# One core, cross-attention and a soft mixture of experts: queries as two products (x by Wq, then by turned Wk, two heads side by side) in place of one product with both weights multiplied per head

## What is computed

```
h   = layernorm(x)
q   = h @ Wq;  k = ctx @ Wk;  v = ctx @ Wv          (16 heads of 64)
x   = x + softmax(q k^T / 8) v @ Wo
x   = x + softmoe(layernorm(x))                     (64 experts x 32 slots)
```

## Time and profile before

| | us |
|---|---|
| median of 3 runs (lowest, highest) | 438.74 (438.14, 440.42) |
| the profiled execution, its own time | 439.33 |
| its span in the profile | 437.5 |
| first scores of half 0 / of half 1 / of half 2 start at | 14.92 / 57.40 / 104.41 |

### The profile page before, as it was taken

One profiled execution on the slowest core, in us unless ns is written; L12 is line 12 of the kernel. 1 busy time (PEld: TensorE's weight loads), 2 busy tenths in 40 slices (PEclk: granted clock), 3 DMA queues, 4 the chain that ended last, 5 costly groups with the idle time before them and its releaser, 6 DMA issues.

```text
span 437.5 us, 7430 instructions
## 1 busy us (share of the span) xinstructions
PE 423.5 (97%) x2994; PEld 385.7 (88%) x2994; DVE 331.7 (76%) x608; ACT 245.4 (56%) x413; POOL 160.4 (37%) x89
## 2 busy tenths in 40 slices
PE   6999999999999999999999999999999999899997
PEld 4788899999999999889999998899999888788987
DVE  2777757766786768767898689978988999659870
ACT  2575565675466456645663766456656565534641
POOL 2509900506050305031707053617140342456740
PEclk8999999999999999999999999999999999999999
DMA  8211020114011001210011011001000000196000
GB/s 232 74 51 15 4 82 17 21 63 114 14 23 61 19 13 14 72 18 14 13 72 20 12 14 70 19 12 15 0 20 14 9 4 18 38 254 192 1 1 22
DMA packets 15198, 19.05 MB, mean 44 GB/s; under 512 B 4042, under 2 KB 10970, under 8 KB 15164
## 3 DMA queue, kind: packets, MB, share of 16 engines
q1 hardware_dynamic: 13294, 15.98, 14.4%
q10 hardware_dynamic: 1870, 2.60, 2.1%
HBM read 18.32 MB, written 0.26 MB: 42 GB/s over the span
## 4 chain that ended last, share of the span: by engine, by line
PE 76%; DVE 11%; ACT 5%; issue 2%; POOL 2%; DMA 2%; POOLq 1%; ACTq 0%
PE turned L691 15%; PE scores L675 8%; PE acc L713 8%; PE acc L711 8%; PE acc L712 8%; PE scores L681 8%; PE scores L678 8%; PE misc L728 3%; DVE pT_l L1366 3%; DVE small L1356 3%; PE misc L753 2%; ACT prob L1114 2%; PE misc L595 2%; DMA wk_sb<-in_L_xattn_Wk_dram 2%; ACT pT_h L1107 1%
## 5 line engine op out<-in xcount | busy, mean ns | idle before, releaser
L1107 ACT CAST pT_h<-turned 125x512 fp32r<-125x512 f32 x168 | 95.2, 591 | 122.7 <-PE turned L691 122.0
L1366 DVE TENSOR_TENSOR pT_l<-turned,pT_h 125x512 fp32r<-125x512 f32 x168 | 112.3, 687 | 65.5 <-ACT pT_h L1107 64.6
L1356 DVE TENSOR_REDUCE small<-scores 128x1 f32<-128x500 f32 x168 | 108.4, 674 | 6.4 <-PE scores L681 6.0
L691 PE MATMUL turned<-ident,prob 128*125 128x128 f32 x672 | 94.4, 276 | 3.7 <-DVE pT_l L1366 3.5
L691 PEld LDWEIGHTS turned<-ident,prob 128*125 128x125 f32 x672 | 87.5, 187 | 11.2 <-DVE pT_l L1366 5.5
L711 PE MATMUL acc<-pT_h,ctx_nh 125*128 125x256 f32 (+1 forms) x288 | 94.1, 327 | 0.0
L1114 ACT ACTIVATE prob<-scores,small 128x1500 f32<-128x1500 f32 x56 | 85.0, 1518 | 13.0 <-DVE small L1359 12.6
L713 PE MATMUL acc<-pT_h,ctx_nl 125*128 125x256 f32 (+1 forms) x288 | 86.5, 300 | 0.0
L712 PE MATMUL acc<-pT_l,ctx_nh 125*128 125x256 f32 (+1 forms) x288 | 86.3, 300 | 0.0
L675 PE MATMUL scores<-ctx_th,qk_h 128*128 128x500 f32 x168 | 67.9, 404 | 1.4 <-ACT prob L1114 1.4
L681 PE MATMUL scores<-ctx_th,qk_l 128*128 128x500 f32 x168 | 65.4, 389 | 0.0
(11 more groups left out here) (188 smaller groups left out, 544.0 us busy)
## 6 DMA issues: line engine op xcount, KB each, us to landing
ctx_raw<-in_ctx_dram SPq DMA_DIRECT2D x7, 750.0 KB
rbc<-rden_row SPq DMA_DIRECT2D x15, 128.0 KB, 3.1
rbc<-rden_row SPq DMA_DIRECT2D x8, 192.0 KB, 3.0
eb<-in_L_ffn_expert_b_dram SPq DMA_DIRECT2D x4, 256.0 KB, 5.5
ctx_raw<-in_ctx_dram ACTq DMA_DIRECT2D x3, 224.0 KB
wq_sb<-in_L_xattn_Wq_dram ACTq DMA_DIRECT2D x1, 512.0 KB, 5.0
wv_sb<-in_L_xattn_Wv_dram ACTq DMA_DIRECT2D x1, 512.0 KB, 7.0
wo_sb<-in_L_xattn_Wo_dram ACTq DMA_DIRECT2D x1, 512.0 KB, 8.1
```

Of the source, the lines that this page charges most:

```text
L691: last = tr(turned[0:CK, m, 128 * c:128 * c + 128], prob[u][:, CK * j:CK * j + CK], ident[:, :])
L1107: nc.scalar.copy(pT_h[0:CK, PLACES[g // NT % 2][t], CPB * k:CPB * k + CPB, :], turned[0:CK, (KB * u + k) % 2, :].rearrange("p (c r) -> p c ...
L1356: m = v.tensor_reduce(bankmax[:, u, k:k + 1], scores[:, k, 0:KW], AX.X, ALU.max)
L1366: v.tensor_tensor(pT_l[0:CK, place, dst, :], turned[0:CK, (KB * u + k) % 2, :].rearrange("p (c r) -> p c r", c=CPB), pT_h[0:CK, place, dst ...
```

## The change

Wk is turned (with the scale folded in) and Wq stays as it is. The queries come from two products: `make_qT` makes x by Wq for a pair of heads (128 rows, 112 columns), a copy brings it to SBUF, and `make_qk` multiplies each half of 64 rows by the turned Wk of its head; the two heads of a pair use the upper and the lower half of the array and write to two banks. The rounds are pairs 0-1, 2-3 and 4-7, three in place of four. The queries of the other batches are made in the same two steps: `ahead_queries(j)` (three products), a high and a low part taken by ACT and DVE (`hi_queries`, `lo_queries`), then `ahead_heads(j)` (three pairs of products of 64 rows), and `copy_heads(j)`. They start in step 4 of half 0 and end in step 5 of half 1. Before `ahead_queries(0)`, and before `ahead_heads` in steps 2 to 4 of half 1, TensorE waits for a count of `ctxT_lo`, the semaphore of `lo_ctx`. Wk is loaded first and whole by ACT's queue, Wq in two halves; two filler products (`keep_busy`) stand after the turning of Wk. `turn_weight(wv_sb, 1)` and its copy move from step 1 to step 2. The core of the diff:

```diff
-        wqk, wqk_at = take("wqk", [D, HEADS, D])
+        wq_sb, wqk_at = take("wq_sb", [D, INNER])
+        wkT, _ = take("wkT", [128, HEADS // 2, D])
...
+        QK_PAIRS = ((0, 2), (2, 4), (4, 8))
+
         def rounds_of_qk(t):
 
-            return min(4, -(-(-(-128 * (t + 1) // T)) // 4))
+            heads = -(-128 * (t + 1) // T)
+            return 1 + sum(heads > 2 * j1 for _, j1 in QK_PAIRS[0:-1])
+
+        def qk_banks(r):
+
+            j0, j1 = QK_PAIRS[r]
+            two = turned if r == 0 else misc
+            return two[:, :, 0:PT * (j1 - j0)].rearrange("p m (h b t) -> p b h m t", b=2, t=T)
+
+        def heads_of(ap, r):
+
+            j0, j1 = QK_PAIRS[r]
+            return ap[:, 2 * j0:2 * j1, :].rearrange("p (h m) t -> p h m t", m=2)
...
             sp.dma_start(x_sb[:, :, :], x_v).then_inc(x_in, 16)
-            sp.dma_start(wk_sb[0:DH, :], Wk[0:DH, :]).then_inc(wk_in, 16)
+            sp.dma_start(wq_sb[0:DH, :], Wq[0:DH, :]).then_inc(wq_in, 16)
...
+                    pool.wait_ge(qk_lo, len(QK_PAIRS))
+                    pool.wait_ge(qk_cp, len(QK_PAIRS))
...
-                pool.wait_ge(setup_act, 5)
-                pool.wait_ge(setup_dve, 3)
+                pool.wait_ge(wq_in, 32)
+                pool.wait_ge(setup_act, 1)
+                pool.wait_ge(setup_dve, 1)
                 pool.wait_ge(xnT_dve, 2)
-                gp.tensor_tensor(wqk_h[:, :, :], wqk[:, :, :], zero[:, :].unsqueeze(2).broadcast_to([D, HEADS, D]),
-                                 ALU.add).then_inc(wqk_hi, 1)
+                zeros = zero[:, :].broadcast_to([128, INNER])
+                wkT_cols = [w[:, :, :].rearrange("p j d -> p (j d)") for w in (wkT, wkT_h, wkT_l)]
+                gp.tensor_tensor(wq_h[:, :], wq_sb[:, :], zeros, ALU.add)
+                gp.tensor_tensor(wkT_cols[1], wkT_cols[0], zeros, ALU.add).then_inc(wsplit_hi, 1)
                 gp.tensor_tensor(xa_h[:, 0:PT], xnT[:, 3 * PT:4 * PT], zero[:, :].broadcast_to([D, PT]), ALU.add)
                 gp.tensor_tensor(xa_h[:, PT:NA], xnT[:, PT:3 * PT], zero[:, :].broadcast_to([D, 2 * PT]),
                                  ALU.add).then_inc(xa_hi, 1)
-                pool.wait_ge(wqk_hi, 1)
-                gp.tensor_tensor(wqk_l[:, :, :], wqk[:, :, :], wqk_h[:, :, :].bitcast(F32),
-                                 ALU.subtract).then_inc(wqk_lo, 1)
+                pool.wait_ge(wsplit_hi, 1)
+                gp.tensor_tensor(wq_l[:, :], wq_sb[:, :], wq_h[:, :].bitcast(F32), ALU.subtract)
+                gp.tensor_tensor(wkT_cols[2], wkT_cols[0], wkT_cols[1].bitcast(F32),
+                                 ALU.subtract).then_inc(wsplit_lo, 1)
...
+            def make_qT(j0, j1, k):
+
+                for j in range(j0, j1):
+                    last = mm(bank(k)[:, PT * (j - j0):PT * (j - j0) + PT], wq_sb[:, 128 * j:128 * j + 128],
                               xnT[:, 0:PT], start=True, stop=True)
-                last.then_inc(qk_pe, 1)
-
-
-            def ahead_head(h, m):
-
-                o = misc[:, m, 0:NA]
-                mm(o, wqk_h[:, h, :], xa_h[:, :], start=True, stop=False)
-                mm(o, wqk_h[:, h, :], xa_l[:, :], start=False, stop=False)
-                mm(o, wqk_l[:, h, :], xa_h[:, :], start=False, stop=True).then_inc(ahead_pe, 1)
+                last.then_inc(setup_pe, 1)
+
+            def make_qk(r):
+
+                j0, j1 = QK_PAIRS[r]
+                two = turned if r == 0 else misc
+                for j in range(j0, j1):
+                    for m in range(2):
+                        p = slice(DH * m, DH * m + DH)
+                        last = mm(two[:, m, PT * (j - j0):PT * (j - j0) + PT], wkT[p, j, :], qT[p, j, :],
+                                  start=True, stop=True)
+                        if j == j1 - 1:
+                            last.then_inc(qk_pe, 1)
+
+            def ahead_queries(j):
+
+                o = misc[:, 1, 0:NA]
+                cols = slice(128 * j, 128 * j + 128)
+                mm(o, wq_h[:, cols], xa_h[:, :], start=True, stop=False)
+                mm(o, wq_h[:, cols], xa_l[:, :], start=False, stop=False)
+                mm(o, wq_l[:, cols], xa_h[:, :], start=False, stop=True).then_inc(aq_pe, 1)
+
+            def ahead_heads(j):
+
+                i = j % 2
+                pe.wait_ge(aq_lo, j + 1)
+                for n, (w, q) in enumerate(((wkT_h, qa_h[i]), (wkT_h, qa_l[i]), (wkT_l, qa_h[i]))):
+                    for m in range(2):
+                        p = slice(DH * m, DH * m + DH)
+                        last = mm(misc[:, m, 0:NA], w[p, j, :], q[p, :], start=(n == 0), stop=(n == 2))
+                        if n == 2:
+                            last.then_inc(ahead_pe, 1)
...
             pe.wait_ge(ident_ready, 1)
             keep_busy(2)
-            pe.wait_ge(wq_in, 16)
-            turn_weight(wq_sb, 0, S0)
-            turn_weight(wq_sb, 1, S1)
-            pe.wait_ge(wk_in, 32)
+            pe.wait_ge(wk_in, 16)
             turn_weight(wk_sb, 0, S2)
             turn_weight(wk_sb, 1, T0)
+            keep_busy(2)
             pe.wait_ge(xn_ready, 1)
-            turn_xn(0, 1)
+            turn_xn(0, 1, ACC)
+            pe.wait_ge(wq_in, 32)
+            pe.wait_ge(xnT_dve, 1)
+            make_qT(0, 2, T1)
             turn_ctx(0, 0, 1, first=True)
-            pe.wait_ge(setup_act, 3)
+            pe.wait_ge(setup_act, 2)
             pe.wait_ge(setup_dve, 1)
-            head_pairs(wqT, wkT, 0, T1, S0)
+            make_qk(0)
             turn_ctx(0, 1, 0, first=True)
-            pe.wait_ge(setup_act, 4)
-            pe.wait_ge(setup_dve, 2)
-            pe.wait_ge(xnT_dve, 1)
-            make_qk(0, ACC)
             pe.wait_ge(ctxT_lo, 1)
             turn_ctx(0, 2, 1, first=True)
...
                 q = (b - 4) // 2
-                if b == 1 and t == 0:
-                    pe.wait_ge(wqk_lo, 1)
-                    pe.wait_ge(xa_lo, 1)
-                    ahead_head(0, 0)
-                    ahead_head(1, 1)
-                if b == 1 and 1 <= t <= 5:
-                    pe.wait_ge(ahead_act, 2 * t + 2)
-                    ahead_head(2 * t + 2, 1)
-                if b == 1 and t == 5:
-                    pe.wait_ge(ctxT_lo, KB * (b + 2))
-                    ahead_head(13, 0)
+                if b == 1 and t <= 5:
+                    if 2 <= t <= 4:
+                        pe.wait_ge(ctxT_lo, KB * (b + 1) + t - 1)
+                    ahead_heads(t + 2)
...
+                if b == 1 and t <= 4:
+                    pe.wait_ge(ahead_act, t + 3)
+                    ahead_queries(t + 3)
...
                     if first:
                         if t == 0:
-                            make_qk(1, M0)
-                            head_pairs(wqT, wkT, 2, T0, T1)
+                            make_qT(2, 4, ACC)
                             pe.wait_ge(qk_lo, 1)
                             pe.wait_ge(qk_cp, 1)
+                            make_qT(4, 8, T0)
+                            pe.wait_ge(setup_act, 3)
+                            make_qk(1)
                             pe.wait_ge(xn_ready, 2)
-                            turn_xn(1, NQ)
+                            turn_xn(1, NQ, T1)
                         if t == 1:
-                            pe.wait_ge(xnT_dve, 2)
                             pe.wait_ge(wvo_in, 32)
                             turn_weight(wv_sb, 0, ACC)
                             pe.wait_ge(qk_lo, 2)
                             pe.wait_ge(qk_cp, 2)
-                            turn_weight(wv_sb, 1, M0)
-                            make_qk(2, M1)
+                            make_qk(2)
                         if t == 2:
-                            pe.wait_ge(setup_dve, 4)
-                            make_qk(3, M0)
-                            pe.wait_ge(setup_act, 6)
                             pe.wait_ge(qk_lo, 3)
                             pe.wait_ge(qk_cp, 3)
+                            turn_weight(wv_sb, 1, M0)
+                            pe.wait_ge(setup_act, 4)
                             head_pairs(wvT, wo_sb, 0, ACC, M1)
                         if t == 3:
-                            pe.wait_ge(qk_lo, 4)
-                            pe.wait_ge(qk_cp, 4)
+                            pe.wait_ge(setup_dve, 3)
                             turn_ctx(1, 0, 0)
-                            pe.wait_ge(setup_act, 7)
-                            pe.wait_ge(setup_dve, 5)
+                            pe.wait_ge(setup_act, 5)
+                            pe.wait_ge(setup_dve, 4)
                             head_pairs(wvT, wo_sb, 2, ACC, M1)
                         if t == 4:
-                            pe.wait_ge(setup_dve, 6)
+                            pe.wait_ge(setup_dve, 5)
                             turn_ctx(1, 1, 1)
                             pe.wait_ge(ctxT_lo, KB + 1)
                             turn_ctx(1, 2, 0)
-                            pe.wait_ge(setup_act, 8)
...
```

(98 more changed lines are left out.)

121 lines of the change are left out of this document (46 added, 75 removed).

## The result

| | before | changed |
|---|---|---|
| median, us (lowest to highest) | 439.24 (438.14 to 440.42) | 450.86 (447.76 to 454.39) |
| ratio to before, 95% interval | | 1.0244 (1.0201 to 1.0287) |
| the profiled execution, its own time / span | 439.33 / 437.5 | 454.39 / 451.9 |
| first scores of half 0 / half 1 / half 2 | 14.92 / 57.40 / 104.41 | 14.62 / 63.78 / 118.84 |

The direction was right and the size wrong: +4.65 was forecast, +11.6 came, and 450.9 lies above the range's end of 448.5. Two of the signs of being wrong came too: first scores after 13.5, and a granted clock under 1.0 after 15 us. The profiled execution is the slowest of the four, so what it shows is the upper end.

What follows compares the result with a forecast made beforehand. TensorE, busy 97% of the span, was taken as the bound, so a new wait costs its length. Terms -2.9 + 0.4 + 2.75 + 1.3 - 0.9 + 5.4 - 1.4 = +4.65 on 438.74 gave 443.4, range 439.8 to 448.5.

Steps and rivals of the forecast that it cites:

- signs of being wrong: Half 1 steps 2 to 4 within 0.5 of today's lengths; first scores after 13.5; granted clock under 1.0 after 15 us.
- 1, first scores: Setup ahead of the first scores: they come at about 12.0, gain 2.9; 1.4 if the clock falls, not over 3.3.
- 2, half 0 steps 0 to 3: Step 0: 0, step 1: -0.2, step 2: +0.4, step 3: +0.3; sum +0.4 (bounds -0.3 and +1.2).
- 3, step 4: End of half 0 step 4: ahead_queries(0) waits 2.3 for the first lo_ctx, plus three products; +2.75 (1.8 to 3.3).
- 4, steps 5, 6: Half 0 steps 5 and 6 get ahead_heads and ahead_queries, a pair priced as one product: +0.3 and +1.0.
- 5, half 1 steps 0, 1: Step 0: two pieces in place of four heads, -0.9; step 1: two pieces for two heads, 0.
- 5, steps 2 to 4: Half 1: ahead_heads in mid_step waits about 1.8 for lo_ctx of the same step, three times; +5.4.
- 5, step 5: Half 1 step 5: one piece in place of four heads; -1.4.
- the clock behind the waits: Rival: clock falls in the four new waits, 1.5 us lost at each; +6, 449.4; chance 0.12.
- the price of the pair form: Rival: eight half-array pieces, entering and leaving at 0.1 each; +1.6, 445.0; chance 0.10.
- that rival's 447.2: Rival: the pairs run one after the other, each piece 0.47 more; +3.75, 447.2; chance 0.07.
- The rival on the other side: Rival: waits cover slack in TensorE's list; without the four, -3.05, 435.7; chance of faster 0.06, half-way 0.14.

Runs made afterwards that it cites:

- e10_after_again: The changed kernel once more, unedited, for more executions and a second profile; median 449.5 us, ratio 1.0216.
- e4_fill_three: The changed kernel with two filler products in each of the three waits of half 1, the waits kept; 448.4 us, ratio 1.0206.
- e6_before_three_waits: The kernel before, with TensorE made to wait for lo_ctx in half 1, steps 2 to 4; 445.2 us, ratio 1.0132.
- e3_both_late: As e1_heads_late, and ahead_queries(0) moved from step 4 of half 0 to step 5, with pieces 0 to 2 placed later; 443.7 us, ratio 1.0095.
- e1_heads_late: The changed kernel with ahead_heads of half 1, steps 2 to 4, moved behind the first part of the context product; 444.3 us, ratio 1.0114.
- e8_full_array: As e1_heads_late, but each pair of 64-row products is one product over all 128 rows; 442.5 us, ratio 1.0073.

## Why the prediction was right in sign and wrong in size

Changed kernel at full clock (steps of e10_after_again and e4_fill_three) less before, by the prediction's parts:

| part | predicted | measured |
|---|---|---|
| 1, first scores | -2.9 | -0.3 in the profile; -1.4 as a mean of profiles |
| 2, half 0 steps 0 to 3 | +0.4 | +0.7 |
| 3, step 4 | +2.75 | +2.92 |
| 4, steps 5, 6 | +0.3, +1.0 | +0.25, +1.25 |
| 5, half 1 steps 0, 1 | -0.9, 0 | -0.54, +0.3 |
| 5, steps 2 to 4 | +5.4 | +6.18 |
| 5, step 5 | -1.4 | -0.98 |
| the clock behind the waits | 0 | +2.8 to +4.1 (median; +2.5 to +3.7 by ratios), +4.7 (profile) |

The sum of parts 2 to 5 is 10.1, not 7.55. With part 1 and the clock the profile comes to -0.3 + 10.1 + 4.7 = 14.5 (14.4 by the spans), and the median to 11.2 to 12.8 (+11.6). Three terms failed: the gain of part 1 (2.9 forecast, 0.3 to 1.4 measured), the price of the pair form, put at nothing (2.3), and the clock behind the waits, put at nothing (2.5 to 4.1).

**Right:** the bound by TensorE, so that a wait costs its length (5.65 for three in e6_before_three_waits); the four waits, their place and what ends them (predicted 1.8 and 2.3; 1.6 and 2.4 in the profile); pairs side by side (x2 at one start), so that rival's 447.2 fell; POOL's split was in time (it ends at 41.96, and TensorE waits for `lo_ctx` until 47.1).

**Part 1 was mis-sized.** It compared a new setup without a slow part with the one profile of before, which had run a part at the low level. Without a slow part the kernel before begins its scores at 13.5 (e6_before_three_waits) and the changed one at 11.8, a gain of 1.7; where a part is slow, the old one begins at 14.9 and 14.8 and the changed one at 14.6 and 14.8, a gain near 0. Over seven profiles of the changed setup the mean is 13.0, over four of the old (one with fillers) 14.4. The bound of 1.4 holds the mean, not the 0.3 of the profile. I had allowed for one thing, a fall of the clock behind the turning. What came is another: in the two late profiles (the changed kernel's and e3_both_late) the first load is there at 6.7 and 6.5, where the first turn starts at 5.2 to 5.9 in the ten others, and turns and fillers are slow at a granted clock of 1.00. I had taken that landing as fixed. That the first fillers' 3.45 was a low clock no row shows either (the granted clock is 1.00 from 1.6 to 5 us); that later ones take about half of it, 1.88 in e1_heads_late, holds.

**Parts 4 and 5 left out the price of the half-array form.** It stood as a rival at 0.1 for entering and 0.1 for leaving. In the kernel before, the eight turns begin 0.79 ahead of the head and the head takes 0.55:

```profile
74.65 1.04 PE L691 MATMUL turned<-ident,prob 128*125 128x128 f32 x8
```

In the changed one the turns begin 0.97 ahead and the piece takes 0.66:

```profile
73.62 1.03 PE L735 MATMUL turned<-ident,prob 128*125 128x128 f32 x8
74.59 0.42 PE L656 MATMUL misc<-qa_h,wkT_h 64*128 64x336 f32 x2
...
75.25 0.39 PE L755 MATMUL acc<-pT_h,ctx_nh 125*128 125x256 f32 x1
```

That is 0.29, and with a slower start of the next product 0.3 to 0.4, as e8_full_array measured in most steps. Over the five pieces without a wait beside them that is some 1.7, and 0.2 more at each of the other three (6.18 with pairs against 5.65 with the waits alone): 2.3 in all. That rival was true and its 1.6 too small. Without the form the steps 0, 1 and 5 of half 1 come to -0.94, +0.12 and -1.38, near the -0.9, 0 and -1.4 forecast. So the form is most of the 2.5 between 7.55 and 10.1, though not term by term: part 2 was 0.3 too low, part 3 0.2 and the three waits 0.25, while the work of part 4 without its form was put too high. The Trainium skill (TensorEngine Tiling (Array Packing), Key Properties) says that changing the tiling mode drains TensorE. The trace agrees that the change costs time, 0.3 to 0.4 us a piece; that it is a drain no run here shows. I gave it a chance where it should have stood in the sum, since each entry had a row.

**The clock was a rival** at 0.12, priced 6 us; it happened in most executions, for 2.8 to 4.1. The argument against it, that the halves are full of dense work, was no row. The range had room for the form alone (445.0) or the clock at its measured price alone; at its full 6 us (449.4) the clock alone lay outside already. With both true at once, and part 1 short by 1.5, the time leaves the range.

**The rival on the other side** fell: a wait's cover by slack is 0 in half 1. Only in step 4 some 1.0 came back in the next step, and that in the kernel before.

## What to carry to other kernels

Before work is moved within a list that one engine fills, look for which bank it writes and when the last reader of that bank is due in another engine's list; here that alone told four waits of 7 us. A saving on paper of a full product by two half-array ones isn't one when it is cut into pieces among full-size work: each piece, entered and left, cost 0.3 to 0.4 us. And add up rivals that can be true together, above all a wait and the clock that may fall behind it.

## What was not expected of the hardware

The clock fell behind waits of 1.6 and 2.4 us in the changed kernel, and six executions of the kernel before with three waits of 1.7 had no lower mean clock than without them. In the changed kernel itself the same waits had it in one profile and not in another. Over the twelve profiles it fell behind two of six idle pauses of 2.4 (step 4 of half 0), two of nine of 1.6 (half 1) and two of twelve of 1.4 (378 to 393 us); the kernel before had none behind three of 1.7 and one of 2.3 in those places. What decides this beyond the length of the pause is not settled by these runs. A stretch at the low level cost 1.5 to 1.6 us each time (8.38 against 6.81, 10.46 against 8.92, 9.71 against 8.14). And the setup of any profile needs a second look: two executions of one kernel began their first scores at 12.6 and 14.6, at a granted clock of 1.00 in both.
